# An attention loop on one core: one pair of batches in its body, or three

## The reference

```python
def rmsnorm(x, g, eps=EPS):
    var = jnp.mean(jnp.square(x), axis=-1, keepdims=True)
    return x * jax.lax.rsqrt(var + eps) * g
...
q = (hidden_states @ Wq).reshape(B, Sq, H, D)
k = (encoder_hidden_states @ Wk).reshape(B, Skv, H, D)
v = (encoder_hidden_states @ Wv).reshape(B, Skv, H, D)
q = rmsnorm(q, gq)
k = rmsnorm(k, gk)
scores = jnp.einsum('bqhd,bkhd->bhqk', q, k) * scale
attn = jax.nn.softmax(scores, axis=-1)
out = jnp.einsum('bhqk,bkhd->bqhd', attn, v)
return out.reshape(B, Sq, H * D) @ Wo
...
x = x + jnp.tanh(g_xattn[0]) * _L0_xattn_ref(_layernorm(x, axis=-1), ctx_1024, ...)
x = x + jnp.tanh(g_ffn[0]) * _L0_ffn_ref(_layernorm(x, axis=-1), ...)
```

## Time and profile before

| | |
|---|---|
| median of 3 runs | 2559.78 us (2559.45 to 2561.59) |
| the profiled execution | 2562.17 us |
| its span, first to last instruction | 2560.4 us |
| mean granted TensorE clock | 0.966 of 2.4 GHz |
| busy: TensorE, VectorE, ScalarE, GpSimd | 90%, 75%, 63%, 48% |
| attention loop on TensorE | from 110.8 to 2063.0 us |

### The profile page before, as it was taken

The page is one execution under the profiler, slowest core; times in us unless marked ns, Lnnn a source line. Parts: engine busy times, 40 slices in busy tenths (PEclk is TensorE's granted clock), DMA queues, the critical chain, the costliest instruction groups (busy, mean ns, idle before and its releaser), DMA issues. The chain is left out here.

```text
span 2560.4 us, 53642 instructions
## 1 busy us (share of the span) xinstructions
PE 2306.1 (90%) x16826; PEld 1620.0 (63%) x16826; DVE 1924.2 (75%) x4239; ACT 1602.3 (63%) x3290; POOL 1218.5 (48%) x1537
## 2 busy tenths in 40 slices
PE   3699999999999999999999999999999997399998
PEld 2477767676767677776767676767676775244443
DVE  4577777787777777777777777777777775569996
ACT  3566767676766666666666666666666674654443
POOL 4356565555555656555555555555555552000000
PEclk8799999999999999999999999999999999699999
DMA  5455555555555564545465646464646453524443
GB/s 182 114 97 109 105 104 108 100 113 98 116 92 122 89 116 91 120 91 117 92 122 91 122 88 123 86 123 90 125 86 123 88 111 71 218 55 118 107 118 96
DMA packets 837287, 277.40 MB, mean 108 GB/s; under 512 B 797584, under 2 KB 809136, under 8 KB 836528
## 3 DMA queue, kind: packets, MB, share of 16 engines
q1 hardware_dynamic: 837040, 274.08, 52.1%
HBM read 63.21 MB, written 13.11 MB: 30 GB/s over the span
## 5 line engine op out<-in xcount | busy, mean ns | idle before, releaser
L1023 POOL TENSOR_TENSOR ksplit<-khat,ksplit 128x512 bf16<-128x512 f32 (+1 forms) x384 | 449.8, 1173 | 103.4 <-ACT ksplit L551 103.3
L763 DVE TENSOR_TENSOR khat<-keys_ps,krs 128x512 f32<-128x512 f32 (+1 forms) x384 | 263.5, 686 | 284.4 <-POOL krs L1017 284.4
L1014 POOL TENSOR_SCALAR kvar<-kss 128x4 f32<-128x4 f32 (+1 forms) x384 | 84.7, 220 | 680.4 <-DVE kss L753 680.4
L1017 POOL TENSOR_TENSOR krs<-kvar,minus_half 128x4 f32<-128x4 f32 (+1 forms) x384 | 387.1, 1008 | 32.0
L556 ACT ACTIVATE ksq<-keys_ps 128x512 f32<-128x512 f32 (+1 forms) x384 | 228.8, 597 | 254.6 <-PE keys_ps L25 254.6
L571 ACT ACTIVATE early<-score_ps,nbias,qrs 100x361 f32<-100x361 f32 x512 | 330.5, 651 | 89.7 <-DVE nbias L781 87.2
L23 PE MATMUL keys_ps<-wk_hi,ctxT_hi 128*128 128x512 bf16 (+1 forms) x768 | 301.9, 393 | 67.9 <-issue 36.2
L580 ACT ACTIVATE psplit<-early,rden 100x361 bf16<-100x361 f32 x512 | 304.6, 595 | 59.9 <-DVE rden L787 58.9
L793 DVE SCALAR_TENSOR_TENSOR psplit<-early,rden,psplit 100x361 bf16<-100x361 f32 x512 | 311.6, 619 | 5.7 <-ACT psplit L580 3.7
L771 DVE TENSOR_REDUCE nmax<-score_ps 100x1 f32<-100x361 f32 x512 | 269.3, 526 | 55.9 <-PE score_ps L25 55.6
L753 DVE TENSOR_REDUCE kss<-ksq 128x4 f32<-128x512 f32 (+1 forms) x384 | 260.1, 677 | 54.6 <-ACT ksq L556 43.1
(11 more groups left out here) (156 smaller groups left out, 5421.2 us busy)
## 6 DMA issues: line engine op xcount, KB each, us to landing
ctx_raw<-in_ctx SPq DMA_DIRECT2D x32, 256.0 KB, 3.1
xin<-in_x SPq DMA_DIRECT2D x32, 200.0 KB
xres<-in_x SPq DMA_DIRECT2D x32, 200.0 KB
x_rows<-xres SPq DMA_DIRECT2D x32, 200.0 KB
xin<-x_rows SPq DMA_DIRECT2D x25, 256.0 KB, 2.9
xres<-x_rows SPq DMA_DIRECT2D x25, 256.0 KB, 2.6
out<-xres SPq DMA_DIRECT2D x25, 256.0 KB, 2.7
kT<-ksplit SPq DMA_TRANSPOSE x384, 3.1
```

The lines of the kernel that those rows point to most:

```text
L763: dve.tensor_tensor(khat[0:KV[t], k, :].rearrange("p (h d) -> p h d", h=G), keys_ps[k][0:KV[t], :].rearrange("p (h d) -> p h d", h=G), rs, ...
L1017: pool.tensor_tensor(krs[0:KV[t], k, :], kvar[0:KV[t], k, :], minus_half[0:KV[t], 0:G], ALU.pow).then_inc(krs_done, 1)
L1023: pool.tensor_tensor(ksplit[0:KV[t], t, 1, :], khat[0:KV[t], (u + t) % 2, :], ksplit[0:KV[t], t, 0, :], ALU.subtract).then_inc(k_lo_done, 1)
```

## The change

The loop's body holds three pairs one behind the other, and the loop runs 5 times. The pair index i becomes three times the loop's register plus 0, 1 or 2. What each engine executes for a pair, and in which order, stays as it was; the peeled last pair too. The same edit is made for all five engines.

```diff
+    BODY = 3
+    assert (PAIRS - 1) % BODY == 0
...
-            with sp.Fori(0, PAIRS - 1) as i:
-                for u in range(1, UNITS + 1):
-                    turn(i, u, False)
+            with sp.Fori(0, (PAIRS - 1) // BODY) as j:
+                for i in (j * BODY + r for r in range(BODY)):
+                    for u in range(1, UNITS + 1):
+                        turn(i, u, False)
...
-            with eng.Fori(0, PAIRS - 1) as i:
-                for u in range(1, UNITS, 2):
-                    two_turns(i, u, False)
+            with eng.Fori(0, (PAIRS - 1) // BODY) as j:
+                for i in (j * BODY + r for r in range(BODY)):
+                    for u in range(1, UNITS, 2):
+                        two_turns(i, u, False)
```

## The result

Three pairs in the loop's body take **2545.58 us** (median of 6 runs, 2540.73 to 2554.74), the kernel before on the same chip 2559.66 (6 runs, 2558.24 to 2562.33): the ratio is 0.9947, 95% interval 0.9929 to 0.9966, faster by 14.1 us or 0.55%. Forecast were 2529 us and a gain of 30.5. So the sign was right, the gain is less than half of what was forecast, and the median lies 0.6 us outside the range (2518 to 2545). The runs spread over 14.0 us, the kernel before over 4.1; in later sessions the kernel before spread over 11.6 us too, so nothing rests on that. The profiled execution is the slowest of the six (2554.74 us, span 2552.9): what its trace gains over the trace of before (7.5 us of span) is less than what the medians gain.

A forecast was written before the change was run, and what follows sets the result against it. TensorE, 90% busy, was taken to set the pace, standing still at its loop's back edges. Terms -35.2 + 2.0 + 1.0 + 1.7 = -30.5 us gave 2529.3 us on the median's scale, range 2518 to 2545 (80%).

The forecast's parts named there:

- back edge costs 3.52 us: TensorE's attention loop: each taken back edge costs 3.52 us (2.81 to about 4.0); ten removed gain 35.2 us.
- the clock: Mid-pair falls of the granted clock: 3 among the ten freed pairs in place of 2.1, +1.7 us, bounds -3.6 and +13.4.
- the "issue" wait: TensorE's unnamed wait ahead of the first keys matmul: to fall from 36.2 us to 10.4 in 4 pieces.
- my 4.3: ScalarE, GpSimd and SyncE, with tripled bodies, were each expected to stall some 4.3 us at the four kept edges.
- the slower rival: Sequencers: if each threshold needs two operations and TensorE's sequencer has no slack, 42.7 us are added, 2572 us; 3%.
- the one by instruction count: Rival: stalls belong to the number of instructions, not the jump, so nothing changes, 2560 us; 3%.
- the index arithmetic costs nothing: Wait thresholds: index is three times the counter plus a constant, still one operation, costed at nothing.
- the two terms of SyncE: SyncE's late key transposes: 2.0 us at the four kept edges, 1.0 us at the ten freed joints.
- my bound of 7.2: Four kept edges: upper bound of SyncE's 2.0 us term, 4 x 1.8 us of third key transpose lateness.
- my bound of 5: Ten freed joints: upper bound of SyncE's 1.0 us term, taken as 0.1 us each, transposes just in time.
- the control joint: Behind the 15th pair, no jump taken: 17.00 us from closing transposes to query squares, no new wait seen.
- everything late at once: Rival: SyncE late by its bounds (5 + 7.2 us), clock down in most pairs (+11): 2548 us, up to 2555; 8%.

The follow-up runs named there:

- the run with the hint: Kernel before, one pair per body, with a prefetch hint for the closing branches on TensorE and VectorE: 2531.74 us, ratio 0.9892.
- the same edits: Later context loads plus five zero-weight matmuls around query squares: 2524.21 us with three pairs per body, 2501.91 us with all fifteen in one body.
- the loads later: Changed kernel, but SyncE issues the next pair's four context loads one turn later, behind the first key transposes: 2527.16 us, ratio 0.9855.
- the repeated run: The changed kernel, three pairs per body on all engines, measured once more: 2551.59 us, ratio 0.9951 against the kernel before.
- two variants: Three pairs per body on TensorE and VectorE alone (2543.28 us, ratio 0.993), and on all engines but SyncE (2544.64 us, ratio 0.9926).
- the two runs with SyncE short: SyncE kept one pair per body; three on TensorE and VectorE alone (2543.28 us), or on all engines but SyncE (2544.64 us).

## Why the prediction was wrong in its size

**Right.** TensorE sets the pace, and its back edge costs 3.52 us: ten joints take 17.09 us in place of 20.5 (the ten pairs, cleared of what SyncE and the clock add, 126.2 in place of 129.8), and the "issue" wait fell to 10.6 us. The mechanism is the fetch of the branch's target (the run with the hint), and straight code does not stall (the run with fifteen pairs). ScalarE, GpSimd and SyncE stall at the kept edges as forecast, at 2.9, 5.7 and 3.6 us for my 4.3. That ScalarE's and GpSimd's stalls are hidden holds too (the run with SyncE alone left short). Each threshold still takes one operation (109 arithmetic operations on TensorE's sequencer in a pair, 110 before), so the slower rival is false, and so is the one by instruction count. That the index arithmetic costs nothing is true only of the change: straight code, which has none of it, takes 125.80 us for a pair where the body of three takes 126.08 with the same edits, some 4 us in fourteen pairs. That the arithmetic is the cause was not isolated.

**Wrong: the two terms of SyncE.** I named the mechanism (key transposes that land late for ScalarE's ksplit write) and gave it 2.0 + 1.0 us.

- *The issues are spaced wider than I took.* "At some 1.3 us each" puts the third issue 2.6 us behind the first. The line that I read this from the earlier trace rows has 5.32 us for the three, which puts the third some 4.1 behind: a misreading. After the change it went 3.0 to 3.5 us behind the first at the kept edges and 3.2 to 5.3 at the freed joints.
- *Kept edges: 2.0 us forecast, 12.1 measured* (4 x 3.03), above my bound of 7.2. At the edge shown the first transpose went at 19.9 us where I had worked out 19.1, and the third 3.4 behind it; so it landed at 26.6 and not at 25.2, and ScalarE stood 3.1 us where I had 1.8. The larger error is the next step: "I take 0.5 us of it per edge as reaching TensorE", for the reason that ScalarE is idle for a third of a pair. At this spot it has no slack: ScalarE's four waits come to 11.8 us, and TensorE loses as much. At the edge shown TensorE meets 1.0 us as a wait for kT, 0.7 as a wait for ScalarE and 0.4 as a wait for VectorE's oT_lo; I could not name the rest. A share of idle time over a whole pair says nothing about one spot of it.
- *Freed joints: 1.0 us forecast, about 9 measured* (ten times 127.04 - 126.18 = 0.86, the clean pairs of the kernel after against those with the loads later; 6.7 by the clean pairs of the repeated run, 126.85), above my bound of 5. I took SyncE to be just in time, with a margin of 0.2 us. The first transpose went even earlier than I had worked out (13.0 to 13.2 us against 13.6), but the third at 17.2 in the median against 16.2, and it landed at 20.5 against 19.6, where ScalarE wants it at 19.8. I also looked at the first 17 us behind the control joint alone; at the freed joints ScalarE's wait ends 20 to 22 us behind the transposes, and at the kept edge shown 26.7.

**Wrong in small: the clock.** In the profile four freed pairs had a fall where I had taken three. My own row spoke for more: of the four pairs without a fall at their edge two had one later, which for ten pairs is five. What I had missed as well is that their number varies from execution to execution (in ten freed pairs four here, two in the repeated run, six in two variants) and that the first pair can have them. Whether that makes the spread of the times is not shown.

With the measured terms the forecast's sum becomes -35.2 + 12.1 + 8.6 = -14.5 us, against 14.1 measured on the medians. That this fits so well is in part luck: the terms come from the slowest of six executions, and the sum leaves out the clock. In that execution the ten freed pairs gain 24.3 us (35.2 less 8.6 for SyncE and some 3 for the added falls, and 0.7 more than forecast), the four others lose 12.1, and 5.6 us are lost ahead of the first closing transposes; its span is 7.5 us shorter than before, for it lies 9.2 us above its median.

The rival *everything late at once* came closest (SyncE's bounds of 5 + 7.2 us and the clock down in most pairs: 2548). I gave it 8%, and my range ended below it. Its SyncE part happened, beyond its bounds (12.1 + 8.6 for 12.2); its clock part was +3 in place of +11.

**Open.** Why the clock falls in some mid-pair stretches and not in others that do the same. The runs show where it falls (behind the one-column query squares) and that added work in the waits there keeps it up. Why the two runs with SyncE short gained 4 to 5 us of the 12: in their profiled executions the four pairs give 11.6 and 12.6 us and the freed pairs take 3.6 and 4.8 back, for the most part by the two more falls that each of them had there, so some 8 us stay; why the medians show 4 to 5 was not separated. Where the last 0.3 us of a pair go that straight code saves, and the 0.5 us that a hinted edge costs.

## What to carry to other kernels

Before a loop body is lengthened to save back edges, read for every engine how long it stands behind its own branch, and what each would cost at three times the body: an engine that passed its edge in 0.25 us may stand 3 to 6 us at it afterwards. When the engine that sets the pace gains time, look for whoever feeds it with no margin, here the queue that issues the DMAs, and move what has slack (loads for the next turn) behind what is waited for; that alone was worth some 20 us here after the change and nothing before it. Read a group of issues by its whole length, and not by the length of one. A prefetch hint on the back edge gave more than a body of three did, at a third of the code.

## What the runs showed of the hardware

- Without the hint a taken back edge stalled TensorE 3.75 to 4.25 us over these runs, from its branch to its next operation. VectorE stalled 3.7 to 4.9 us when TensorE's taken branch lay beside its own, and 3.0 us at the ten joints where it alone stalled (the run with TensorE alone tripled; at the four edges where both stalled, 4.1 to 4.7). With three pairs in the body ScalarE stalled 2.5 to 2.9 us, SyncE 3.0 to 3.9, GpSimd 5.0 to 6.0. With the hint TensorE's branch took 0.45 us.
- Short bodies pass freely: ScalarE's with 307 records of the trace (busy and sequencer) per pair, SyncE's with 169 and GpSimd's with 163 go on after some 0.25 us. VectorE's with 371, GpSimd's tripled (485), SyncE's tripled (499) and ScalarE's tripled (917) do not.
- A mid-pair fall of the granted clock from 1.00 to 0.50 (2.4 to 1.2 GHz) lasts 3.4 us; pairs with one are 1.65 us longer in the kernel after (128.69 in the mean, without 127.04), 1.2 with the loads later and 2.1 in the repeated run. In the loop of the kernel after it came behind sixteen one-column matmuls, ahead of which the engine had waited 0.37 us, and zero matmuls around them removed it.
